# A graph network on one core: six blocks a turn, keys written by ScalarE, more buffers for nodes and projections, and one attribute product of 512 columns

## The reference, cut to what matters

```python
row, col = src, dst                                   # layer 0
h = concat([x[row], x[col], edge_attr_2], -1) @ W1 + b1
h = relu((h - mean(h, 0)) * rsqrt(var(h, 0) + eps) * gamma + beta)
sums = segment_sum(h @ W2 + b2, row, N)
x = layernorm(x + sums / (counts(row) + 1)[:, None] + x)
deg = segment_sum(1, dst) + 1; dinv = rsqrt(deg)      # layer 1, self loops added
conv = lambda h, W, b: segment_sum((h @ W)[src] * (dinv[src] * dinv[dst])[:, None], dst, N) + b
x = layernorm(x + conv(relu(conv(relu(conv(x, W0, b0)), W1, b1)), W2, b2))
```

## Time and profile before

| | |
|---|---|
| median of 3 executions | 4016.34 us (4011.32 to 4021.29) |
| the profiled execution | 4023.21 us, its span 4021.3 us |
| TensorE, busy share of the span | 94% |
| VectorE | 65% |
| ScalarE | 32% |
| mean granted clock of TensorE | 0.98 |

### The profile page before, as it was taken

The page is one execution under the profiler, slowest core; times in us unless marked ns, Lnnn a source line. Parts: engine busy times, 40 slices in busy tenths (PEclk is TensorE's granted clock), DMA queues, the critical chain, the costliest instruction groups (busy, mean ns, idle before and its releaser), DMA issues.

```text
span 4021.3 us, 106978 instructions
## 1 busy us (share of the span) xinstructions
PE 3787.2 (94%) x44274; PEld 2777.1 (69%) x44274; DVE 2611.3 (65%) x3706; ACT 1302.5 (32%) x2645; POOL 55.8 (1%) x53
## 2 busy tenths in 40 slices
PE   3699999999998799999999999995999999999999
PEld 3487887787786688888888888883444444444444
DVE  6999999999994588888888888875111101111122
ACT  5244444444443355554555455544000000000000
POOL 0000000000000000000000000000000000000000
PEclk9899999999998899999999999997999999999999
DMA  6123222222224633333333333332666566656664
GB/s 235 51 82 96 83 81 94 84 82 90 88 82 154 101 131 131 123 129 128 123 131 131 120 131 127 124 136 71 197 197 195 186 202 195 197 179 209 208 209 137
DMA packets 397856, 547.84 MB, mean 136 GB/s; under 512 B 175759, under 2 KB 335256, under 8 KB 390584
## 3 DMA queue, kind: packets, MB, share of 16 engines
q1 hardware_dynamic: 391000, 537.80, 42.2%
q10 hardware_dynamic: 6624, 6.42, 0.5%
HBM read 434.64 MB, written 109.53 MB: 135 GB/s over the span
## 4 chain that ended last, share of the span: by engine, by line
PE 65%; DVE 23%; issue 8%; DMA 2%; ACT 1%; SPq 1%; DVEq 0%; ACTq 0%
PE py L1571 29%; PE ph L1288 10%; PE ph L1290 10%; PE pSum L1304 10%; DVE prod_raw L1109 8%; DVE ring_raw L1082 7%; PE ph L1284 3%; DVE q L1134 1%; DVE q L1137 1%; DVE q L1129 1%; DVE rank L1144 1%; DVE q L1139 1%; PE pY L831 1%; SPq L1238 1%; PE pg L1559 1%
## 5 line engine op out<-in xcount | busy, mean ns | idle before, releaser
L1571 PE MATMUL py<-ring_raw,p 128*128 128x512 bf16 (+1 forms) x3822 | 786.4, 368 | 23.7 <-DVE dummy L1732 21.7
L1290 PE MATMUL ph<-q,prod_raw 128*128 128x128 bf16 x7056 | 781.1, 220 | 1.4 <-issue 1.4
L1288 PE MATMUL ph<-p,prod_raw 128*128 (+1 forms) x7056 | 780.6, 220 | 0.0
L1571 PEld LDWEIGHTS py<-ring_raw,p 128*128 128x128 bf16 x3822 | 362.8, 98 | 438.9 <-DVE dummy L1732 22.1
L1339 ACT ACTIVATE x<-ph 128x512 bf16<-128x512 f32 x588 | 351.1, 597 | 675.6 <-PE ph L1290 667.5
L1284 PE MATMUL ph<-wvb,x 128*128 128x128 bf16 x2352 | 515.6, 219 | 20.9 <-DVE prod_raw L1419 11.9
L1431 DVE SCALAR_TENSOR_TENSOR ring_raw<-ph,x 128x512 f32<-128x512 f32 x588 | 404.0, 687 | 185.2 <-ACT x L1339 178.8
L1288 PEld LDWEIGHTS ph<-p,prod_raw 128*128 128x128 bf16 x7056 | 494.2, 98 | 42.1 <-issue 3.0
L1304 PE MATMUL pSum<-x,ring_raw 128*128 128x384 bf16 x2401 | 499.6, 327 | 6.1 <-DVE x L1436 6.1
L831 PE MATMUL pY<-p,ring_raw 128*128 128x128 bf16 x7203 | 501.0, 219 | 0.5 <-issue 0.5
L1290 PEld LDWEIGHTS ph<-q,prod_raw 128*128 128x128 bf16 x7056 | 495.5, 98 | 1.5 <-issue 1.5
(11 more groups left out here) (314 smaller groups left out, 3937.9 us busy)
## 6 DMA issues: line engine op xcount, KB each, us to landing
ring_raw<-at_dram SPq DMA_DIRECT2D x252, 896.0 KB, 4.8
prod_raw<-lrow_dram SPq DMA_DIRECT2D x147, 768.0 KB, 4.2
at_dram<-ring_raw SPq DMA_DIRECT2D x49, 1568.0 KB, 5.6
prod_raw<-lrow_dram SPq DMA_DIRECT2D x49, 832.0 KB, 4.4
arow_dram<-x SPq DMA_DIRECT2D x147, 73.5 KB
x<-arow_dram SPq DMA_DIRECT2D x147, 54.0 KB
q<-q_dram SPq DMA_DIRECT2D x1, 4704.0 KB, 25.6
ring_raw<-at_dram SPq DMA_DIRECT2D x21, 224.0 KB, 2.5
```

Of the source, the lines that this page charges most:

```text
L1288: nc.tensor.matmul(bank[:, k * P:(k + 1) * P], T[q][:, 0, at:at + P], p_b[:, :, m3, :].rearrange("p a d -> p (a d)"), start=False, stop=False)
L1290: last = nc.tensor.matmul(bank[:, k * P:(k + 1) * P], T[q][:, 1, at:at + P], q3[:, c, m3, :], start=False, stop=m3 == 2)
L1571: last = nc.tensor.matmul(py[par][:, 0:w], g3[c % 2][:, 7 * i + m, k, :], ring[i][:, 0:w // P, m, :], start=i == m == k == 0, stop=i == m ...
```

## The change

It has these parts:

- `drive` takes the number of steps in a turn; TensorE's loop has six (seven turns), the others keep two.
- ScalarE writes the keys: `known[:, g, t, :]` holds the key of edge t for t up to the edge's own place, and -1 beyond (preset once). VectorE compares `known` with the pair's keys in one operation. `key_2`, `same`, the product with `earlier` and the constant `earlier` go.
- `q3st` has four buffers; SP stores q parts ahead of p and q in each turn. The stores of the fourth buffer count on the semaphore `pf_in`, and its later waits are raised by 48.
- In the set-up, signs and weights are made before the sample count, TensorE forms the counts inside its projection loop at g = 2, and `own_cross` runs two groups behind.
- The attribute product of a group is one product over all its columns (512) in place of one for each target block (128).
- The node stage has three `cg` and two `r_inv`; VectorE's order in a turn is left, variance, taken, third, scaled; ScalarE's is middle part, root, squares, copy, high part, x1.

```diff
-            def drive(eng, step):
+            def drive(eng, step, body=2):
...
-                with eng.Fori(0, LOOPED // 2) as k:
-                    for h in range(2):
-                        step(k * 2 + (FIRST + h), k + (FIRST + h) // 2, (FIRST + h) % 2, True, True, True, True, True)
+                with eng.Fori(0, LOOPED // body) as k:
+                    for h in range(body):
+                        step(k * body + (FIRST + h), k * (body // 2) + (FIRST + h) // 2, (FIRST + h) % 2, True, True, True, True, True)
...
-                    drive(pe, step)
+                    drive(pe, step, 6)
...
@@ ScalarE, act_1, step
                         if bkt:
+                            act.wait_ge(S["key_ready"], s + 1)
+                            for g in range(TG):
+                                n = 2 * g + 1
+                                nc.scalar.activation(known[:, g, 0:n, :], key[:, 0:n].unsqueeze(2).to_broadcast([P, n, 2]), ACT.Copy)
+                            odd = known.rearrange("p g t u -> p (g t u)")[:, 3::2 * TPB + 4]
+                            nc.scalar.activation(odd, key[:].rearrange("p (g u) -> p u g", u=2)[:, 1, :], ACT.Copy).then_inc(S["known_ready"], 1)
                             act.wait_ge(S["base_ready"], s + 1)
...
@@ VectorE, dve_1, step
-                            V.scalar_tensor_tensor(out=key[:], in0=rec[u][:, 1, :], scalar=block, in1=rec[u][:, 0, :], op0=ALU.is_equal, op1=ALU.mult)
-                            twice = lambda f: rec[u][:, f, :].unsqueeze(2).to_broadcast([P, TPB, 2])
-                            keyed = mark(V.scalar_tensor_tensor(out=key_2[:], in0=twice(1), scalar=block, in1=twice(0), op0=ALU.is_equal, op1=ALU.mult))
-                            after(keyed)
+                            V.scalar_tensor_tensor(out=key[:], in0=rec[u][:, 1, :], scalar=block, in1=rec[u][:, 0, :], op0=ALU.is_equal, op1=ALU.mult).then_inc(S["key_ready"], 1)
+                            dve.wait_ge(S["key_ready"], s + 1)
...
-                            dims = [P, TG, TPB, 2]
-                            same = mark(V.tensor_tensor(sel[:, :, B:SEL, :], key_2[:].unsqueeze(1).to_broadcast(dims), pairs.to_broadcast(dims), ALU.is_equal))
...
-                            after(same)
-                            counted = mark(V.tensor_tensor(sel[:, :, B:SEL, :], sel[:, :, B:SEL, :], earlier, ALU.mult))
+                            dve.wait_ge(S["known_ready"], s + 1)
+                            counted = mark(V.tensor_tensor(sel[:, :, B:SEL, :], known, pairs.to_broadcast([P, TG, TPB, 2]), ALU.is_equal))
...
@@ TensorE, pe_1
-                    pe.wait_ge(S["dve_start"], COUNTED)
-                    nc.tensor.matmul(pbk[:, 0:B], onesb[:], count_b[:], start=True, stop=True).then_inc(S["pe_start"], 1)
...
                     for g in range(13):
+                        if g == 2:
+                            pe.wait_ge(S["dve_start"], COUNTED)
+                            nc.tensor.matmul(pbk[:, 0:B], onesb[:], count_b[:], start=True, stop=True).then_inc(S["pe_start"], 1)
+                        if g >= 2:
+                            own_cross(g - 2)
                         project(g, g % 2, g - 1 if g >= 2 else 0)
-                        if g >= 1:
-                            own_cross(g - 1)
+                    own_cross(11)
                     own_cross(12)
...
@@ SP, sp_1 (the same block moved ahead of the stores of p and q)
-                            sp.dma_start(q3_dram[:, 4 * g:4 * g + w, :, :], q3st[g % 3][:, 0:w, :, :]).then_inc(q3_out[g % 3], 16)
+                            sp.dma_start(q3_dram[:, 4 * g:4 * g + w, :, :], q3st[g % 4][:, 0:w, :, :]).then_inc(q3_sent[g % 4], 16)
...
@@ TensorE, pe_2, hidden
+                        w = len(group(g))
+                        nc.tensor.matmul(bank[:, 0:w * P], at_rows[u][:, g, :], wvb[:, 0:w, :].rearrange("p k d -> p (k d)"), start=True, stop=False)
                         for k, c in enumerate(group(g)):
-                            nc.tensor.matmul(bank[:, k * P:(k + 1) * P], at_rows[u][:, g, :], wvb[:, k, :], start=True, stop=False)
...
-                                last = nc.tensor.matmul(bank[:, k * P:(k + 1) * P], T[q][:, 1, at:at + P], q3[:, c, m3, :], start=False, stop=m3 == 2)
+                                last = nc.tensor.matmul(bank[:, k * P:(k + 1) * P], T[q][:, 1, at:at + P], q3[:, c, m3, :], start=False, stop=m3 == 2 and k == w - 1)
...
@@ VectorE, dve_3, node stage
-                    if j >= 2:
-                        dve.wait_ge(S["x1_made"], j - 1)
+                    if j >= 3:
+                        dve.wait_ge(S["x1_made"], j - 2)
...
-                    if j >= 1:
-                        dve.wait_ge(S["x1_made"], j)
-                    newton(link, sm[4][:, 0:nb], sm[2][:, 0:nb], sm[3][:, 0:nb])
+                    if j >= 2:
+                        dve.wait_ge(S["x1_made"], j - 1)
+                    newton(link, r_inv[j % 2][:, 0:nb], sm[2][:, 0:nb], sm[3][:, 0:nb])
...
                 for s in range(15):
-                    if s < 13:
-                        taken(s)
                     if 0 <= s - 2:
                         left(s - 2)
                     if 0 <= s - 1 < 13:
                         variance(s - 1)
+                    if s < 13:
+                        taken(s)
```

More of the change, by code:

```diff
@@ L665, in build @@
                 in_x1 = Carve(x1_f[:, X1_FREE:].bitcast(BF16))
-                earlier = in_x1.take(TG * TPB * 2).rearrange("p (g t u) -> p g t u", g=TG, t=TPB)
+                known = in_x1.take(TG * TPB * 2).rearrange("p (g t u) -> p g t u", g=TG, t=TPB)
                 cells = [in_x1.take(9 * BW).rearrange("p (f b) -> p f b", f=9) for u in range(2)]
@@ L681, in build @@
                 offs_f = sb("offs_f", [1, B]); offs = sb("offs", [1, B], I32)
[L682 removed]
+                key = sb("key", [P, TPB], BF16); base_2 = sb("base_2", [P, B, 2], BF16); rank = sb("rank", [P, TPB], BF16)
                 t7 = [sb(f"t7{u}", [P, 7]) for u in range(2)]
@@ L685, in build @@
                 q3st = [sb(f"q3st{u}", [P, 4, 3, D], BF16) for u in range(2)] + [q3_flat[:, NF * COLS:NF * COLS + 12 * D].rearrange("p (b m d) -> p b m d", b=4, m=3)]
+                q3st.append(in_x1f.take(6 * D).bitcast(BF16).rearrange("p (b m d) -> p b m d", b=4, m=3))
+                q3_sent = q3_out + [S["pf_in"]]
                 dummy = sb("dummy1", [P, 1])
@@ L940, in act_1 @@
                             act.wait_ge(S["res"], 2 * g)
-                            nc.scalar.activation(q3st[(g - 1) % 3][:, 0:w, 1, :], rq[u][:, 0:w, :], ACT.Copy).then_inc(S["mid"], 1)
+                            nc.scalar.activation(q3st[(g - 1) % 4][:, 0:w, 1, :], rq[u][:, 0:w, :], ACT.Copy).then_inc(S["mid"], 1)
                     def evacuate(s, m, par):
@@ L1000, in dve_1 @@
                     link(V.memset(lo_all[:, :, B:BW], 0.0))
+                    link(V.memset(known, -1.0))
                     for u in range(2):
@@ L1057, in dve_1 @@
                             dve.wait_ge(S["mid"], 2 * g + 2)
-                            V.tensor_tensor(q3st[g % 3][:, 0:w, 2, :], rq[u][:, 0:w, :], q3st[g % 3][:, 0:w, 1, :], ALU.subtract).then_inc(S["low"], 1)
+                            V.tensor_tensor(q3st[g % 4][:, 0:w, 2, :], rq[u][:, 0:w, :], q3st[g % 4][:, 0:w, 1, :], ALU.subtract).then_inc(S["low"], 1)
                         if i < 13:
@@ L1069, in dve_1 @@
                             dve.wait_ge(S["hi"], 2 * g + 2)
-                            V.tensor_tensor(rq[u][:, 0:w, :], qst[u][:, 0:w, :], q3st[g % 3][:, 0:w, 0, :], ALU.subtract).then_inc(S["res"], 1)
+                            V.tensor_tensor(rq[u][:, 0:w, :], qst[u][:, 0:w, :], q3st[g % 4][:, 0:w, 0, :], ALU.subtract).then_inc(S["res"], 1)
                     dve.wait_ge(S["low"], 26)
@@ L1075, in dve_1 @@
                     dve.wait_ge(proj_out[1], 32 * 6)
-                    for u in range(3):
-                        dve.wait_ge(q3_out[u], 16 * (5, 4, 4)[u])
+                    for u in range(4):
+                        dve.wait_ge(q3_sent[u], 16 * (4, 3, 3, 3)[u])
                     def one_hot(to, of, pairs_):
@@ L1483, in build @@
             x_rest = early_g[:, 0:ROWS - 1536]
-            cg = [early_g[:, ROWS - 1536 + u * 1024:ROWS - 512 + u * 1024].rearrange("p (b d) -> p b d", b=4) for u in range(2)]
-            sm = [sb(f"sm{u}", [P, 4]) for u in range(6)]; ssq = [sb(f"ssq{u}", [P, 4]) for u in range(2)]
+            cg = [early_g[:, ROWS - 1536 + u * 1024:ROWS - 512 + u * 1024].rearrange("p (b d) -> p b d", b=4) for u in range(3)]
+            sm = [sb(f"sm{u}", [P, 4]) for u in range(6)]; r_inv = [sm[4], sb("r_inv", [P, 4])]; ssq = [sb(f"ssq{u}", [P, 4]) for u in range(2)]
             pa = [ps(f"pa{u}", [P, 512]) for u in range(2)]; pb = ps("pb", [P, 512]); pg = ps("pg", [P, 512])
@@ L1617, in act_3 @@
                         for m in range(nb):
```

(2 more changed lines are left out.)

64 lines of the change are left out of this document (31 added, 33 removed).

## The result

The kernel after takes 3986.8 us (median of four runs, 3981.7 to 3988.7) against 4015.9 us before (4011.3 to 4021.3): a ratio of 0.9925, 95% interval 0.9908 to 0.9942. The gain is 29 us; I had forecast 64.5 us and 3952 us.

The account below looks back on a forecast made before the run. VectorE was taken to bound the block loop, with TensorE 0.72 us a step behind. Gains of 27.5 (block loop) + 4.2 + 4.9 + 27.9 = 64.5 us from 4016.3 gave 3952 us, range 3938 to 3988.

Parts of the forecast that it names:

- What bounds the kernel: Block loop: VectorE leads and TensorE follows 0.72 us a step behind, which caps what a faster VectorE can give.
- The keys' part: Block loop: less key work on VectorE gains 35.3 us, less 3.7 us of TensorE stall from ScalarE's new copies.
- break-even of 2.32: Block loop: time in us for ScalarE's 18 copies a step above which TensorE stalls in its third group; 2.4 was forecast.
- 3.7 us of stall: Block loop: TensorE waits 0.08 us a step over 46 steps because ScalarE's copies take 2.4 us.
- Six blocks a turn: TensorE's block loop: six returns with a 3.83 us branch, mostly hidden, lose 4.1 us; bounds 0 to 23 us.
- branch in full: Rival, block loop: six returns cost 3.8 us each with none hidden, 3971 us; chance 8%.
- half-late ScalarE: Rival, block loop: ScalarE's copies take near 3 us, costing 0.7 us a step, 3979 us; chance 14%.
- Attribute product: Second loop: one 512-column product in place of four gains 4.2 us; bounds 0 to 6.
- Projection: Set-up: a fourth q3st buffer gains 4.3 us and signs and weights moved ahead 0.6, together 4.9; bounds 2 to 6.
- Node stage: Node stage: a turn from ga to ga falls from 8.04 to 5.57 us, gaining 27.9 us; bounds 18 to 31.
- The rival in which TensorE sets it: Rival, node stage: TensorE, cold after each pause, makes a turn 6.5 us, 3962 us; chance 12%.
- Convolutions: The three convolutions, 1217 us: the change touches nothing there, so no gain was counted.

Follow-up runs that it names:

- the one with the added waits: Kernel after with two blocks a turn and signs moved, plus TensorE waiting for its last sum before both taken branches of the second loop: 3958.9 us.

## Why the prediction was right or wrong

**What bounds the kernel: right.** VectorE led the block loop by about 0.7 us a step, and with its load lightened TensorE leads: 22.59 us a step against 22.55 forecast (mean of 43 steps, two blocks a turn; 22.63 in the ordinary steps of after).

**The keys' part: right in mechanism, and closer in size than its terms were.** 35.3 - 3.7 = 31.6 us were forecast; alone it gave 30.8 in the block loop. The copies took 2.15 us in the step shown, so my 2.4 was a little high, and under the break-even of 2.32: no wait of TensorE for ScalarE's later copies shows, only 3.3 us at the products over hot_p in all. So the 3.7 us of stall did not come, and the gross gain was 31 us, not 35.3; the two errors cancelled, which was luck.

The 2.2 us for the copies, an estimate from what the Trainium skill, "ScalarE: Activation LUTs" (section "What ACT_TABLE_LOAD costs"), states of an activation's time, was nearer; the trace agrees with it (2.15).

**Six blocks a turn: wrong, and this is the step that failed.** "I take the dear branch, 3.83 us, for six returns", "4.1 us lost", with 23 us as the upper bound; it cost 34 to 36 us. The price of the branch, 3.83 us, was read in a loop where the DMA engines are idle when the branch starts, and my bounds were multiples of it. In the block loop the target's packet has to share the 16 DMA engines with a 1568 KB store that starts at the same moment. That makes 7.1 us of the branch, so 3.9 us of idle time, and behind it the clock is at its lower level for 3.4 to 6.3 us of work, which I had priced at nothing. With the store out of the way the step holds nearly as written: branch 3.3 to 3.8, idle 0.6 or less, 1.3 us a return against 0.68. The rival "branch in full" (19 us) was nearest, and it too lacked the contention and the clock. The measured 3986.8 us does lie in the wide range of 3938 to 3988, by luck: its upper part was there for a half-late ScalarE (3979), which was not late, and I had put the full branch at 3971.

The Trainium skill, "Runtime: NRT & Kernel Launch" (section "Instruction fetch mechanics"), has a taken branch fetch its target first when that is not in the current window of two pages of the instruction memory, and gives TensorE a memory of 2048 instructions in pages of 256. The trace agrees on the fetch: its packet of 16 KB stands on the instruction queue behind each far branch. It does not agree with a window of two pages on TensorE: the two-block body, some 1,430 instructions long, returns in 0.2 us without a packet. That the packet waits for a data transfer is what these runs add.

**Attribute product: right.** The groups start 1501.36 and 1503.57 in after, 2.21 us apart; over the loop the sums of two blocks are 54.213 us apart in place of 54.387, which is 0.087 x 48 = 4.2 us, as forecast. The stage shows 3.5, but can't tell it: from first to last sum it took 1341.8 to 1350.2 us in the kernels with this product (the one with the added waits aside) and 1343.4 to 1349.9 in those without.

**Projection: most of the gain was there and a wait took it.** From the start of the large set-up product (L1017 before, L1035 after) to the first key it is 71.7 us before and 66.2 after, 5.45 us less. But 1.3 us of that are the signs and weights themselves (29.76 to 31.08 in after), which only moved ahead of that product, so 4.1 us are gained (forecast 4.9); the wait at L935 for a free q3st is gone, as forecast. The signs in their new place wait for the weights' transfer, which I had counted as landed: 3.4 us in after. Moving them back recovered 2.1 us of stage. What is left, and the time at which the first input lands (14.7 to 19.1 us in kernels with much the same start), makes the -1.9 us of this stage no more than a reading.

**Node stage: right in mechanism and size.** 29.2 us against 27.9; 5.43 us a turn against 5.6. The rival in which TensorE sets it did not come: its clock there is 0.92, above the 0.81 of before.

**Convolutions:** their -3.6 us are within what one profiled execution scatters (1212.6 to 1219.0 us).

## What to carry to other kernels

Before a loop body is made longer, ask what a far return costs at that place: the price read in another loop holds only if the same transfers are under way when the branch starts, so put the DMA issues of SyncE beside the branch's start. Here 3.4 us of queued work hid a branch of 3.3 to 3.8 us, and a bulk store that started with the branch undid that; moving the store, or keeping the body short, were worth 27 and 34 us here. And a part of a change that is free while another engine leads can cost its full price once a second part has removed that lead: add up the parts in the state that the whole change leaves.

## What the hardware showed that I had not expected

- An instruction fetch of 16 KB shares the 16 DMA engines with data. Its packet came 0.9 to 1.6 us after the branch with the engines idle, and 3.4 to 4.8 us after it with an 832 or 1568 KB transfer under way; the branch took 3.3 to 4.0 us and 5.75 to 7.1 us. Behind the store it started within 0.01 us of the store's last packet.
- Behind each of the six stalls of 3.9 us the granted clock was at its lower level for 3.4 to 6.3 us of work, so the stall was half as dear again as its idle time (36 us for 23.3). It is not certain to fall: with 3.45 us of idle time, in before with six blocks, it fell behind four of six returns. After 0.6 us it stayed at 1.00.
- A body of 42 blocks that is never left took 2.4 us more in the block loop than 21 turns of two, and six far returns cost 36 us beside the store and 8 without it.
- A run can agree with a wrong theory in all its numbers: emptying the queue moved the branch's start to the end of the store as well.
